# Writing out four looped stages of a routed-expert kernel, and moving the last layer's weight split into its preparation

## What is computed

```python
x = x + L3_conv(_ln_c(x))                      # depthwise 3x3, layer 3
t = _to_tokens(x); flat = _ln_t(t)
probs = softmax(flat @ router_w.T)
topk_probs, topk_idx = top_k(probs, 2)          # normalised to sum 1
h = silu(flat @ w1[e].T) * (flat @ w3[e].T)     # per expert e, 682 wide
y = h @ w2[e].T
t = t + sum over the two experts of gate * y
```

## Time and profile before

| | |
|---|---|
| time, median of 3 runs | 2315.94 us (2314.86 to 2321.67) |
| time of the profiled execution | 2319.88 us |
| its span, first to last instruction | 2318.0 us |
| TensorE busy / VectorE / ScalarE / GpSimd | 70% / 74% / 59% / 43% of the span |
| mean granted TensorE clock | 0.815 |
| indirect DMAs on GpSimd: row writes (L605) | 352, 394.2 us busy |
| indirect DMAs on GpSimd: scatters (L581) | 288, 328.6 us busy |

### The profile page before, as it was taken

The page is one execution under the profiler, slowest core; times in us unless marked ns, Lnnn a source line. Parts: engine busy times, 40 slices in busy tenths (PEclk is TensorE's granted clock), DMA queues, the critical chain, the costliest instruction groups (busy, mean ns, idle before and its releaser), DMA issues.

```text
span 2318.0 us, 50893 instructions
## 1 busy us (share of the span) xinstructions
PE 1612.0 (70%) x16820; PEld 1202.0 (52%) x16821; DVE 1704.9 (74%) x2874; ACT 1361.0 (59%) x2473; POOL 1000.0 (43%) x955
## 2 busy tenths in 40 slices
PE   4367777768676777667667933699924199978995
PEld 3334444435343444336666822588823088867884
DVE  3567767776877677546777878788866588869886
ACT  0256655676778575775555731477711277766774
POOL 1024334432223122882222467244477677754443
PEclk8588857788887676997788965799955599989997
DMA  7000000000001000000000010000020211110002
GB/s 302 0 25 1 1 25 1 1 1 1 1 1 74 25 1 2 22 21 20 17 17 18 27 56 23 23 27 28 22 83 23 93 37 33 34 63 23 27 28 88
DMA packets 53029, 76.27 MB, mean 33 GB/s; under 512 B 14905, under 2 KB 37642, under 8 KB 50206
## 3 DMA queue, kind: packets, MB, share of 16 engines
q1 hardware_dynamic: 30658, 43.26, 5.9%
q0 software_dynamic: 22208, 30.81, 3.8%
HBM read 40.89 MB, written 35.19 MB: 33 GB/s over the span
## 4 chain that ended last, share of the span: by engine, by line
PE 33%; DVE 16%; issue 5%; POOL 5%; ACT 2%; DMA 2%; POOLq 0%; SPq 0%; ACTq 0%; DVEq 0%
PE bank L1634 12%; PE bank L1635 9%; PE bank L1648 5%; POOL rows L581 3%; PE bank L1650 2%; DVE tmp L1083 2%; PE bank L1620 1%; DVE act L1243 1%; DVE hl L1247 1%; PE bank L1388 1%; POOL x L619 1%; PE bank L1530 1%; ACT act L789 1%; DVE st L907 1%; DVE tmp L1060 1%
## 5 line engine op out<-in xcount | busy, mean ns | idle before, releaser
L605 POOL DMA_INDIRECT y<-ysb,ids x352 | 394.2, 1120 | 519.3 <-DVE ysb L1234 446.4
L619 POOL TENSOR_TENSOR x<-x,ysb 128x256 f32<-128x256 f32 x288 | 266.1, 924 | 670.4 <-DVE ysb L1321 661.9
L771 ACT ACTIVATE hb<-bank,bias_sb 128x512 f32<-128x512 f32 x432 | 299.4, 693 | 246.3 <-issue 138.7
L1634 PE MATMUL bank<-xT,gA 128*114 128x256 f16 x1056 | 331.3, 314 | 59.1 <-DVE act L1243 28.5
L581 POOL DMA_INDIRECT rows<-rowsb,pos x288 | 328.6, 1141 | 98.6 <-issue 74.6
L1243 DVE TENSOR_TENSOR act<-bank,act 114x512 f32<-114x512 f32 x352 | 241.6, 686 | 164.1 <-ACT act L789 163.7
L789 ACT ACTIVATE act<-bank 114x512 f32<-114x512 f32 x352 | 210.2, 597 | 234.9 <-PE bank L1635 230.9
L1635 PE MATMUL bank<-xT,uB 128*114 128x256 f16 x1056 | 299.6, 284 | 0.0
L1634 PE MATMUL bank<-xT,uA 128*114 128x256 f16 x1056 | 299.5, 284 | 0.0
L1635 PE MATMUL bank<-xT,gB 128*114 128x256 f16 x1056 | 299.3, 283 | 0.0
L1648 PE MATMUL bank<-dW,hl 114*128 x2112 | 260.1, 224 | 7.1 <-DVE hl L1247 6.2
(11 more groups left out here) (246 smaller groups left out, 3410.6 us busy)
## 6 DMA issues: line engine op xcount, KB each, us to landing
xs<-rows SPq DMA_DIRECT2D x176, 65.0 KB
stage<-up SPq DMA_DIRECT2D x8, 1368.0 KB, 6.6
rows<-land POOLq DMA_DIRECT2D x8, 1137.5 KB, 18.1
y<-ysb,ids POOLq DMA_INDIRECT x352, 2.2
rows<-rowsb,pos POOLq DMA_INDIRECT x288, 2.3
stage<-down SPq DMA_DIRECT2D x2, 1368.0 KB
rowsb<-y SPq DMA_DIRECT2D x4, 640.0 KB, 6.3
rows<-land POOLq DMA_DIRECT2D x4, 585.0 KB, 20.7
```

What stands on the lines that cost most here:

```text
L605: pool.indirect_dma_start(y_d[h], bass.IndirectOffsetOnAxis(ids[h][:, t * SUB + u:t * SUB + u + 1], 0), ysb[t % UNROLL][:, u * C:(u + 1) * ...
L619: pool.tensor_tensor(xv, xv, tg[u % 2], ALU.add).then_inc(s["added"], 1)
L771: ins = a.activation(dst[:, 0:SPAN * P], PB[w % 3][:, :], ACT.Gelu, scale=1.0 / WSCALE, bias=b1T[l][:, at:at + 1])
L1634: pe.matmul(PB[bank][0:CH, o], w[0][:, at], xT[k][:, :], start=True, stop=False)
```

## The change

The nine middle passes are written out in all four wide stages, on ScalarE, VectorE and TensorE; `middle` is gone. On SyncE the row loads stay a loop. The weight split of layer 3 is issued by `beside` at four places in the preparation of (3,1): pieces 0 and 1 ahead of it, piece 2 after the first norm, piece 3 in the middle of the convolution, piece 4 after the second norm. ScalarE's wait for the evictions of (2,1) now stands ahead of that preparation. SyncE loads the second piece with the first, before (2,0), and the others as before behind the return of (2,1)'s rows. `EARLY` is 4.

```diff
-EARLY = 30
+EARLY = 4
...
+        def beside(steps, weights):
+
+            for at, k in ((LN1 - 1, 1), (LN1 + 9, 2), (CONV + 15, 3), (LN2 + 9, 4)):
+                steps.upto(at)
+                weights.upto(WPREP + 3 * k + 2)
+            steps.upto(LAST)
...
             load_stage(2, range(PIECES))
-            load_stage(3, range(1))
+            load_stage(3, range(2))
...
             for l in range(SPARSE, NL):
-                if l == 3:
-                    load_stage(3, range(1, PIECES))
                 for h in range(HALVES):
                     moe(l, h)
                     if (l, h) != (NL - 1, 0):
                         bring(l, h)
+                if l == SPARSE:
+                    load_stage(3, range(2, PIECES))
...
-                if aside is None:
-                    middle(a, body)
-                else:
-                    for i in range(1, LOOPS - 1):
-                        body(i)
+                for i in range(1, LOOPS - 1):
+                    body(i)
...
             moe(2, 1, None)
-            Woven(prep(3, 1)).upto(LAST)
             a.wait_ge(s["y_done"], tile_base(3, 0))
-            Woven(wprep(3)).upto(LAST)
+            beside(Woven(prep(3, 1)), Woven(wprep(3)))
...
             moe(2, 1, None)
-            Woven(prep(3, 1)).upto(LAST)
-            Woven(wprep()).upto(LAST)
+            beside(Woven(prep(3, 1)), Woven(wprep()))
```

More of the change, by code:

```diff
@@ L417, in experts @@
             return {k: eng.snap((w >> (3 * (k + 1))) & (E - 1), min_val=0, max_val=E - 1) for k in tiles}
-        def middle(eng, body):
-            with eng.Fori(1, LOOPS - 1) as i:
-                body(i)
         def split_base(l, h):
@@ L1269, in moe @@
                 body23(0, first=True)
[L1270 to L1274, removed]
+                for i in range(1, LOOPS - 1):
+                    body23(i)
                 body23(LOOPS - 1)
```

## The result

The changed kernel takes 2292.37 us (median of 4 runs, 2290.64 to 2296.98), the kernel before 2315.4 us beside it: a ratio of 0.9899, 95% interval 0.9875 to 0.9923. A second measurement on another occasion gave 2300.04 against 2315.72, 0.9919 (0.9890 to 0.9949). The gain is 23.0 us in the one and 15.7 us in the other, on average 19; forecast were 11.5, so the sign was right and the size too small by some 8 us.

A forecast was written before the change was run, and what follows sets the result against it. Bounds: TensorE's pace per tile, 37 us from routing to first product, and GpSimd's last scatter for (3,1). 3.9 + 22.9 - 18.3 + 3.0 = 11.5 us gained, giving a median of 2304.4 us; range 2282 to 2315.

The forecast's parts named there:

- Loops of (2,1): Writing out the looped passes of layer 2's second half saves 3.9 us, bounds 0 and 4.5.
- Pieces 0 and 1 of the split: At the end of (2,1), two VectorE splits hold GpSimd's last row write, delaying the preparation of (3,1) by 4.9 us.
- the row of 6.46 us: Trace row where a GpSimd DMA instruction beside the same two splits took 6.46 us instead of 0.96.
- Pieces 2 to 4: In the preparation of (3,1), these splits lie where VectorE works without a wait and cost 9.4 us.
- The gap that closes: Between (3,1)'s routing and (3,0)'s first product, removing the split there frees 37.3 us, less 0.1.
- GpSimd in (3,0): More scatters between row writes make GpSimd set the pace at 5.10 us per tile, losing 18.3 us.
- Loops of (3,1): Writing out the looped passes of layer 3's second half saves 3.0 us.
- 5.3 to 5.4 us per tile: Rival: GpSimd's pace in (3,0), or repeated blocking by the split, leaves a gain of 1 to 5 us; chance 0.13.
- 0.07 us more for each of 72 tiles: Extra loop gain by the Trainium skill's instruction-fetch section, some 4.5 us over both stages; left out of the sum.
- fourth step: On GpSimd in (3,0): 68 instead of 42 scatters lie between the row writes, losing 18.3 us.
- TensorE's tiles 4.65 apart: Sign in (3,0) that would show the forecast wrong; it expected GpSimd's row writes 5.1 us apart.
- the rival with the clock: In (3,0), TensorE waiting for GpSimd loses clock; ten slow tiles give -23 us, 2328; chance 0.07.

The follow-up runs named there:

- e1: The kernel before, with only the middle loops of three engines written out: 2307.5 us, ratio 0.9959 to the kernel before.
- e4: The changed kernel with EARLY put back to 30: 2295.2 us, ratio 0.9910 to the kernel before.
- e2: The kernel before, with only the weight split moved into the preparation of (3,1), loops and EARLY 30 kept: 2301.7 us, ratio 0.9941.
- e3: The kernel before with EARLY = 4 instead of 30 and nothing else: 2332.8 us, ratio 1.0074.
- e9: The changed kernel without layer 3's weight split and its loads, so it computes something else: 2289.4 us, ratio 0.9881 to the kernel before.
- e8: The changed kernel with EARLY = 10, scatters over 40 tiles, and split pieces 3 and 4 in a wait of VectorE: 2272.0 us, ratio 0.9797.
- e6: The changed kernel with EARLY = 10: 2289.7 us, ratio 0.9886 to the kernel before.
- e7: The changed kernel with EARLY = 10 and the remaining scatters spread over 40 tiles instead of 44: 2279.2 us, ratio 0.9831.
- e10: The changed kernel, but in (3,0) VectorE writes only 2 of 512 columns of each low part: 2281.6 us, ratio 0.9851.
- e5: The changed kernel again, unchanged, as reference on another occasion: 2300.0 us, ratio 0.9919 to the kernel before.

## Why the prediction was right, and where it was off

By its steps, with the marks of before and after:

- **Loops of (2,1)**: 3.9 forecast, 2.7 measured to the last eviction (218.7 to 216.0) and 2.4 to the start of the last row write (e1: 2.1; e4 against e2: 3.5). The forecast took one written-out pass of 18.5 us against one looped pass of 19.0. The means of eight passes are 18.69 and 19.04, so a pass gives 0.35 and not 0.5 us. The first pass makes the rest of the difference: it takes 25.97 us in the kernel before but 27.06 and 26.86 in e2 and e3, which loop too. The "4.46 against 4.39" within a pass came from one step of each kind; over all steps within the passes it is 4.56 against 4.54.
- **Pieces 0 and 1 of the split**: 4.9 forecast, 1.1 measured. From the last eviction (1689.55 before, 1678.15 after) to the first addition (1701.51, 1691.19) it is 11.96 us before and 13.04 after. The step that failed is the reading of the row of 6.46 us as "held until both splits are over". In the kernel after GpSimd got in between them, and the row write lost only 1.6 us (the item as a whole cost 1.1, and by e9, which has no pieces there, 12.5 us from eviction to addition, about 0.5). Here the rule of the Trainium skill ("SBUF — State Buffer", section "SBUF: two separate sides"), that the loser waits for the end of one instruction, was the better guide; the trace agrees with it, with 2.61 us instead of 6.46, and e9, with 0.98. The forecast had set it aside for a single row. That row isn't chance: e1 and e3, which have the split in the same place as before, show 6.46 us as well, so the rule doesn't hold in every case. The instructions of 6.46 us start 0.3 us after the first split does, those of 2.61 us 1.3 us after it, and in e8 one that starts 0.7 us after the first split of its pair takes 3.16 us and is let in between them too. Whether the time of the start decides it is open.
- **Pieces 2 to 4**: 9.4 forecast, 9.0 measured (first addition to last position, 111.1 before, 120.1 after). e9 confirms the two items together with 9.5.
- **The gap that closes**: 37.2 forecast, 37.3 measured (last position to first row write, 52.4 to 15.2).
- **GpSimd in (3,0)**: 18.3 lost by forecast, 11.4 and 13.7 measured. That GpSimd's chain sets when (3,1) can start was right (e3, e6, e7, e10), the pace of 5.10 us a tile too high: 4.94 and 4.99. This is the largest missed term. The 5.10 was put between 5.03 and 5.18; the upper one came from a single tile of before, whose instructions met VectorE's at a fixed phase (1.25 us for a write), and even the lower took means from that stage. With GpSimd no longer waiting for the eviction, more of its instructions are short: 60 of the 86 row writes between the two marks take about 1.0 us, against 38 before, and the means are 1.09 and 1.08 us instead of 1.12 (1.10 and 1.10 in e5). That they then fall into VectorE's pauses is argued, not shown.
- **Loops of (3,1)**: 3.0 forecast, 1.4 measured.

Sum, with the first item taken to the last eviction, where the second begins: 2.7 - 1.1 - 9.0 + 37.3 - 11.4 + 1.4 = 19.9 us, with rounding the 19.8 of the marks. The range held without luck of much weight: the misses are 3.8, 0.4, 0.1 and 6.9 us in favour of the kernel, 1.2 and 1.6 against it, so they don't cancel but leave the gain 8 us above the forecast.

Three sums of the forecast are slips. Ten tiles at the lower clock would have given 2339 us and not 2328, since the 23 us lost count from the kernel before (2316). 5.3 to 5.4 us per tile give +2.9 to -1.4 us and not 1 to 5. And 0.07 us more for each of 72 tiles are 5.0 us and not 4.5. None of them enters the likeliest case.

One step of the mechanism failed. The forecast said that GpSimd sets TensorE's pace in (3,0), with evictions waiting for buffers, and that TensorE's tiles 4.65 apart would prove it wrong. They are 4.68 apart on average behind the first (46 of 50 us busy), and yet the last scatter came when GpSimd's own chain let it, since GpSimd's lag grows by under 0.3 us per tile and four buffers hide it to the last evictions. Even at the forecast's 5.10 the lag would have grown by only 0.45 us per tile, and TensorE would have met it late in the stage (an estimate from 5.10, 4.65 and four buffers). It isn't TensorE's pace that GpSimd held back, but the start of the next stage. So TensorE's idle time ahead of (3,1) is 22.0 us where the forecast said over 12; the sum of the time isn't touched by this, as it counted GpSimd's chain. And the rival with the clock didn't come: the granted clock is 1.00 in (3,0), and TensorE waited there only at the end.

One part of the change doesn't pay. By e4 and the two profiles after, EARLY = 4 is no gain over 30 beside the other parts; alone it costs 16 us (e3); and 10 is better than 4 by 6 to 8 us by the marks (e6). The forecast had folded this into its fourth step and not priced it as an edit of its own. The parts that pay are the loops (6.3 us by the marks in e1, 8.3 from e2 to e4) and the split (13.2 us in e2).

## What to carry to other kernels

An engine that is busy 43% of the span can set the end: count its instructions between the event that frees it and the event for which the next stage waits, at their pace with issue included, and see whether what others wait for stands last in its queue. Where ring buffers hide a lag, put the work that the next stage needs ahead of the work that only has to be done. And put moved work where its engine waits, not merely where another one is idle: the same two splits, 6.4 us long, cost 5.9 us less in VectorE's wait than in the middle of its work.

## What was not expected of the hardware

- Two VectorE instructions of 2.96 us one behind the other held a GpSimd DMA instruction of 0.96 us for 6.46 us in the kernel before, in e1 and in e3, but let one in between them in the kernel after, in e2 and in every later profile with that pair at the end of (2,1) (2.61 us each time).
- The work ahead of (2,1), the same in the kernels of all twelve profiles but for one earlier weight load in some, ends up to 14 us apart from one execution to another (1460.4 to 1474.2 us to the start of (2,1)). For changes of this size a single pair of traces misleads unless it is read from a common mark.
